# Linear attention with a mixture of experts: the attention's weights split by columns instead of by rows, k and q projected ahead of v

## The chip, the cores and the metric

The kernel runs on one core of a Trainium2 chip. The metric is the device time of one execution in microseconds (us). Three runs of the kernel before gave 1036.61, 1034.99 and 1036.34 us, median 1036.34.

## The reference

The input is x with 16 batches of 512 tokens and 256 features. For each batch the kernel computes:

```python
h = layernorm(x)
q, k, v = elu(h @ Wq.T) + 1, elu(h @ Wk.T) + 1, h @ Wv.T      # 16 heads of 16
num_i = q_i @ sum_{j<=i} k_j v_j^T ;  den_i = q_i . sum_{j<=i} k_j
x = x + (num / (den + 1e-8)) @ Wo.T
h = layernorm(x)
# router over 8 experts in 4 groups (best 2 groups, best 4 experts), weights cw
x = x + sum_e cw_e * (silu(h @ Wg_e) * (h @ Wu_e)) @ Wd_e + shared expert
```

## The kernel before, in words

Each batch is one tile: 512 tokens in four groups of 128. Every product of the projections and of the experts is computed with each float32 operand split into a high part and a remainder, three matmuls for one (`product`, line 989: high by high, high by low, low by high). ScalarE (ACT) makes the high part by a copy into a type of fewer bits, and VectorE (DVE) or GpSimd (POOL) the low part, the whole less the high part.

The order of the work on each engine is written out by hand in the tables `FIRST`, `STEP` and `LAST`: a word such as `k.0.0` is the step k, part 0, batch 0. Each engine goes through its own list strictly in order, and a step begins with the waits that its operands need. `FIRST` holds the start of the program and batches 0, 1 and part of 2; `STEP` is the pattern that repeats for batches 3 to 15; `LAST` is the end. The change touches `FIRST` alone.

The weights come as ten "pieces". SyncE's queue (SP) loads each into a staging buffer, ACT writes its high part (line 566), and POOL its low part (line 694), except piece 0, whose low part is DVE's (line 773). Pieces 0 and 1 are the attention's matrix `w_qkvo`, 256 rows in two blocks of 128 by 1024 columns (q, k, v and o, 256 columns each): before, piece n is row block n with all 1024 columns, in `cw_all`. Every projection sums over both row blocks, so each waits for both pieces. Pieces 2 to 6 are the experts' gate and up matrices, 7 to 9 the down matrices. The staging buffers of pieces 2 to 5 are those of `scores`, so no mask step of batch 0 may run before piece 5 has been split.

Steps of batch 0 that the prediction speaks of:

- `ln1_stats` (DVE, lines 749 to 757 and 783): means and variances, here that of batch 1 (`ln1_stats.0.1`), which stands in DVE's list directly ahead of `k.0.0`. After four `bn_stats` come small instructions on 128x4 elements. Three (752, 753, 754) are issued together and end in a wait for the third; then 755 and 756 together and a wait; then 757 and a wait; then 783 and a wait.
- `turn` (PE, line 1042): the normalized x transposed by TensorE; then ACT takes the high part (593) and DVE the low part (797).
- `warm.n` (PE, line 1034): n transposes that nobody reads; `WARM` is the number of such transposes ahead of the list (line 1003).
- `k`, `q` (PE, two row blocks by three matmuls of 512 columns; ACT relu at 624 and exp at 627; DVE at 816 writes `kf` or `qf`) and `v` (PE, twelve matmuls of 256 columns; ACT at 616). k has one scratch half of `expo` for both parts, so ACT's `k.1.0` waits until DVE has finished `k.0.0`; `q.1.0` on PE uses the bank of `q.0.0` and waits for DVE's `q.0.0`.
- `q_split` (ACT, 636), `scores` (PE, 1098), `mask` (DVE 860, or ACT 650 with POOL 720), `cum` (DVE scan, 853), `rstd1` (POOL, 699), which waits for `ln1_stats`.

Of the kernel before, what the change touches and what calls it, by code (L numbers as in the profile page):

```python
# [6 lines left out]
B, S, D = 16, 512, 256  # L7
# [9 lines left out]
KC = D // P  # L17
# [6 lines left out]

ET, HR, CW, SM, XB = 3, 3, 4, 8, 2
BANKS = 6
WARM = 16

# [33 lines left out]
}  # L64
FIRST = {
    "PE": """
        turn.0.0 turn.1.0 warm.17.0 v.1.0 k.0.0 q.0.0 v.0.0 k.1.0 q.1.0 scores.0.0 k_turn.0.0 scores.1.0
        warm.8.0 turn.0.1 turn.1.1 k_turn.1.0 state.0.0 values.0.0 scores.2.0 inter.0.0 values.1.0 scores.3.0
        k.0.1 q.0.1 inter.1.0 state.1.0 values.2.0 values.3.0 q.1.1 inter.2.0 scores.0.1 inter.3.0 warm.10.0
        k.1.1 wo.0.0 wo.1.0 scores.1.1 k_turn.1.1 v.1.1 v.0.1 k_turn.0.1 values.0.1 state.0.1 scores.2.1  # L70
# [3 lines left out]
        k_turn.1.2  # L74
        """,
    "ACT": """
        piece.0.0 piece.1.0 turn.1.0 turn.0.0 piece.2.0 v.1.0 piece.3.0 k.0.0 piece.4.0 piece.5.0 q.0.0 k.1.0
        q_split.0.0 q.1.0 mask.1.0 v.0.0 mask.3.0 k_turn.0.0 ln1_apply.0.1 mask.7.0 piece.6.0 turn.0.1
        turn.1.1 mask.5.0 q_split.1.0 k_turn.1.0 wide.0.0 mask.9.0 mask.11.0 mask.13.0 piece.7.0 mask.15.0
        k.0.1 q.0.1 wide.1.0 at.0.0 q_split.0.1 q.1.1 mask.1.1 mask.3.1 at.1.0 k.1.1 mask.5.1 mask.7.1  # L80
# [160 lines left out]
def linear_attention_moe(nc, x, w_qkvo, w_gate_up, w_down, w_router, bias, consts, out):  # L241
    f32, f32r = mybir.dt.float32, mybir.dt.float32r
    ALU, ACT, AX = mybir.AluOpType, mybir.ActivationFunctionType, mybir.AxisListType

    ctx = ExitStack()
    with ctx:
# [6 lines left out]
        def sem(name):  # L253
            return ctx.enter_context(nc.semaphore(name))


        wa_hi, wa_lo = (sb(f"wa_{n}", [P, KC, 4 * D], f32r) for n in ("hi", "lo"))
# [32 lines left out]
        scores = sb("scores", [P, SM, 4, P])  # L290
# [23 lines left out]
        warm = sb("warm", [P, SUBS])  # L314
# [21 lines left out]
        split_hi = sem("split_hi")  # L336
# [126 lines left out]
        def slot(b, e, n):  # L463
# [5 lines left out]
        staging = ([cw_all[:, 2 * j:2 * j + 2, :].rearrange("p a n -> p (a n)") for j in range(2)]  # L469
                   + [scores[:, 2 * j:2 * j + 2, :, :].rearrange("p a h n -> p (a h n)") for j in range(4)]  # L470
                   + [x_mid[1 - j][:, :, :].rearrange("p s d -> p (s d)") for j in range(2)])
        PIECES = [(w_qkvo[:, kc], 4 * D, wa_hi[:, kc], wa_lo[:, kc]) for kc in range(KC)]
        for s in range(0, SLOTS, 2):
            n = min(2, SLOTS - s)
            PIECES.append((w_gate_up[:, s * GU:(s + n) * GU], n * GU,
# [2 lines left out]
        for s in range(0, SLOTS, 4):  # L478
            n = min(4, SLOTS - s)
            PIECES.append((w_down[:, s * D:(s + n) * D], n * D,  # L480
                           wd_hi[:, s:s + n].rearrange("p s n -> p (s n)"),
                           wd_lo[:, s:s + n].rearrange("p s n -> p (s n)")))
        NP, NS = len(PIECES), len(staging)
        staged = [sem(f"staged{n}") for n in range(NP)]
        GATE_PIECE = [KC + i // 2 for i in range(SLOTS)]
        DOWN_PIECE = [KC + (SLOTS + 1) // 2 + i // 4 for i in range(SLOTS)]

        def wait_split(eng, n):

            if ("piece", n, 0) in SPLIT_DVE:  # L490
                wait_for(eng, attn_split, SPLIT_DVE["piece", n, 0])
            else:
                wait_for(eng, split_lo, SPLIT_POOL["piece", n, 0])
# [3 lines left out]
        @block.sync  # L497
        def _(sp):
            def load_x(b):

                wait_drained(sp, "wo", 0, b - XB)
                wait_drained(sp, "wo", 1, b - XB)
                if b == 0:
                    sp.dma_start(x_in[0][:, 0:HALF, :], x_v[0][:, 0:HALF, :]).then_inc(x_half, 16)
                    sp.dma_start(x_in[0][:, HALF:SUBS, :], x_v[0][:, HALF:SUBS, :]).then_inc(x_loaded[0], 16)
                else:
                    sp.dma_start(x_in[b % XB][:, :, :], x_v[b]).then_inc(x_loaded[b % XB], 16)

            for name, i, b in program("SP"):
                if name == "load_x":  # L510
                    load_x(b)
                elif name == "consts":
                    sp.dma_start(cst[:, :], consts).then_inc(small_in, 16)
                    sp.dma_start(bias_sb[:, :], bias.partition_broadcast(P)).then_inc(small_in, 16)
                    sp.dma_start(wr[:, :, :], w_router).then_inc(small_in, 16)
                elif name == "piece":
                    if i >= NS:
                        wait_split(sp, i - NS)
                    src, cols, _, _ = PIECES[i]
                    sp.dma_start(staging[i % NS][:, 0:cols], src).then_inc(staged[i], 16)  # L520
                elif name == "cw_store":
                    sp.wait_ge(cw_turned, b + 1)
                    for g in range(SUBS):
                        sp.dma_start(cw_dram[b % 2][:, g * P:(g + 1) * P], cw_t[RG * g:RG * g + E, :])\
                            .then_inc(cw_stored, 16)
                elif name == "cw_load":
                    sp.wait_ge(cw_stored, 64 * b + 64)
                    if b == 0:
                        wait_split(sp, NP - 1)
                    e = E * b + i - CW  # L530
                    if e >= 0:
                        wait_weighed(sp, e % E + int(e // E < B - 1), e // E)
                    sp.dma_start(cw_all[:, i % CW, :], cw_dram[b % 2, i].partition_broadcast(P))\
                        .then_inc(cw_loaded[i % CW], 16)
                elif name == "put":
                    sp.wait_ge(blocked, BLOCKED["blocks", i, b])
                    n = 2 * KC * (SUBS - 1) * P // 64 if i == 2 else SUBS * D // 32
                    for g in range(4):
                        rows, cs = slice(32 * g, 32 * g + 32), slice(32 * g, 32 * g + 32)
                        dst = (k_dram if i == 2 else x_dram[i])[b % 2].rearrange("(j t) d -> t j d", t=32)  # L540
                        sp.dma_start(dst[:, :, cs], blocks[rows, 0:32 * n].rearrange("t (j d) -> t j d", d=32))\
                            .then_inc(put_done, 16)
                elif name == "get":
                    sp.wait_ge(put_done, PUT["put", i, b])
                    if i == 2:
                        wait_filled(sp, "state", 0, b - 1)
                        wait_filled(sp, "state", 1, b - 1)
                        sp.dma_start(k_tok[:, :, :, :].rearrange("p m c d -> p (m c) d"),
                                     k_dram[b % 2].rearrange("(n p) d -> p n d", p=P)).then_inc(got[2], 16)
                    else:  # L550
                        sp.dma_start(landed[i].rearrange("p s k n -> p (s k) n"),
                                     x_dram[i][b % 2].rearrange("(n p) d -> p n d", p=P)).then_inc(got[i], 16)
                elif name == "store":
                    for j in range(2):
                        half = slice(j * HALF, (j + 1) * HALF)
                        sp.wait_ge(y_drained, Y_DRAINED["result", 0, b] - 1 + j)
                        sp.dma_start(out_v[b][:, half, :], x_mid[b % 2][:, half, :]).then_inc(out_sent[b % 2], 16)
            sp.wait_ge(out_sent[0], 32 * (B // 2))
            sp.wait_ge(out_sent[1], 32 * (B // 2))

        @block.scalar
        def _(act):
            def weights_high(n):
                _, cols, hi, _ = PIECES[n]
                act.wait_ge(staged[n], 16)
                nc.scalar.activation(hi, staging[n % NS][:, 0:cols], ACT.Copy).then_inc(split_hi, 1)


            act.wait_ge(zeros_set, 1)
# [115 lines left out]
        def _(pool):  # L685
# [4 lines left out]
            for name, i, b in program("POOL"):  # L690
                if name == "piece":
                    pool.wait_ge(split_hi, i + 1)
                    _, cols, hi, lo = PIECES[i]
                    nc.gpsimd.tensor_tensor(lo, staging[i % NS][:, 0:cols], hi.bitcast(f32), ALU.subtract)\
                        .then_inc(split_lo, 1)
                elif name == "rstd1":
                    pool.wait_ge(var1_ready, VAR1["ln1_stats", 0, b])
# [5 lines left out]
                elif name == "take":  # L703
                    pool.wait_ge(taken_hi, TAKEN_HI["take", i, b])
                    dst, hi = (xa_lo, xa_hi) if i < 2 else (xt_lo[b % 2], xt_hi[b % 2])
# [30 lines left out]
        def _(dve):  # L736
# [31 lines left out]

            for name, i, b in program("DVE"):
                if name == "piece":  # L770
                    _, cols, hi, lo = PIECES[i]
                    dve.wait_ge(split_hi, i + 1)
                    nc.vector.tensor_tensor(lo, staging[i][:, 0:cols], hi.bitcast(f32), ALU.subtract)\
                        .then_inc(attn_split, 1)
                elif name == "ln1_stats":
                    if b == 0:
# [17 lines left out]
                elif name == "turn":  # L794
                    dve.wait_ge(turn_hi, TURN_HI["turn", i, b])
                    dst, hi = (xa_lo, xa_hi) if i < 2 else (xt_lo[b % 2], xt_hi[b % 2])
# [22 lines left out]
                elif name == "blocks":  # L819
                    wait_blocks(dve, i, b)  # L820
                    if i == 0:
                        dve.wait_ge(norm1_ready, NORM1["ln1_apply", 0, b])
                        src = expo
                    elif i == 1:
                        dve.wait_ge(norm2_ready, NORM2["ln2_apply", 0, b])
                        src = num_t
                    else:
                        dve.wait_ge(drained[BANK["k", 0]], USES["k", 0, b])
                        dve.wait_ge(drained[BANK["k", 1]], USES["k", 1, b])
                        src = kf  # L830
                    n = (SUBS - 1) * P if i == 2 else S
# [153 lines left out]
        def _(pe):  # L985
# [18 lines left out]
            for name, i, b in program("PE"):  # L1004
# [40 lines left out]
                elif name in ("v", "wo"):  # L1045
# [3 lines left out]
                        wait_at(pe, 0, b)  # L1049
                        wait_at(pe, 1, b)  # L1050
                    if b == 0:
                        for n in range(KC):
                            wait_split(pe, n)
                    src = XA if name == "v" else AT
                    w0 = 2 * D if name == "v" else 3 * D
                    for j in range(2):
# [5 lines left out]
                elif name in ("k", "q"):  # L1062
                    w0 = (D if name == "k" else 0) + i * P
                    wait_normal(pe, 0, b)
                    if b == 0:
                        for n in range(KC):
                            wait_split(pe, n)
                    for kc in range(KC):
                        last = product(bk[:, :], cols(WA, ALL, kc, slice(w0, w0 + P)),
                                       cols(XA, ALL, kc, ALL), kc == 0, kc == KC - 1)  # L1070
# [130 lines left out]
```

## Time and profile before

| | |
|---|---|
| runs | 1034.99, 1036.34, 1036.61 us |
| profiled execution | 1035.56 us, span 1033.8 us |
| busy: PE, DVE, POOL, ACT | 1007.7, 873.0, 537.8, 422.6 us |
| chain that ended last | PE 87%, DVE 6%, DMA 2%, ACT 1%, POOL 1% |

The span runs from the first to the last instruction; 1.76 us of the execution lie around it. Busy time is the time in which the engine had an instruction in work. The chain that ended last is followed back from the last instruction to what released each step.

### The profile page before, as it was taken

To read this page: it belongs to the slowest core of one execution; us is meant where nothing else is said; L and a number is where in the kernel's file an instruction comes from. 1 tells how busy PE (TensorE), PEld (TensorE's weight loads), DVE (VectorE), ACT (ScalarE), POOL (GpSimd) and SP (SyncE) were. 2 spreads that over 40 slices of the span, in tenths; PEclk is the share of its full clock that TensorE was granted. 3 is DMA by queue.
4 is the path that set the end of the run, shared out by engine and by line. 5 is a ranking of instruction groups with operands and counts; after the bars stand their busy time and mean duration, and the time that the engine had idled before them with its cause. 6 is when DMAs were issued, how large, how long until landed. Compare 5 with 4: busy or idle time off the path is not lost.

```text
span 1033.8 us, 22214 instructions
## 1 busy us (share of the span) xinstructions
PE 1007.7 (97%) x8437; PEld 858.1 (83%) x8437; DVE 873.0 (84%) x1855; ACT 422.6 (41%) x750; POOL 537.8 (52%) x440
## 2 busy tenths in 40 slices
PE   6889999999999999999999999999999999999997
PEld 5667878888888888888888888888888888888886
DVE  5988998898888889989898988889889898887564
ACT  5755343443434344343444434244343434422222
POOL 5763545636455564445646454564445546443653
PEclk9999999999999999999999999999999999999999
DMA  5011424444242443324435252443424345241511
GB/s 204 2 47 43 106 60 133 83 103 111 60 138 63 132 105 96 100 63 134 83 103 113 58 138 63 142 94 99 100 64 136 76 103 113 58 118 36 130 60 64
DMA packets 235161, 96.49 MB, mean 93 GB/s; under 512 B 161712, under 2 KB 217520, under 8 KB 235056
## 3 DMA queue, kind: packets, MB, share of 16 engines
q1 hardware_dynamic: 235056, 95.07, 36.0%
q8 instruction: 68, 1.11, 0.5%
q14 instruction: 37, 0.30, 0.1%
HBM read 66.60 MB, written 28.44 MB: 92 GB/s over the span
## 4 chain that ended last, share of the span: by engine, by line
PE 87%; DVE 6%; DMA 2%; ACT 1%; issue 1%; POOL 1%; SPq 1%; DVEq 0%; ACTq 0%
PE bank L989 53%; PE y_bank L989 19%; PE bank L1098 6%; PE bank L1114 5%; PE bank L1085 2%; PE bank L1128 2%; PE bank L1140 1%; DMA cw_all<-cw_dram 1%; DMA cw_all<-in_w_qkvo 1%; DVE scores L860 1%; DMA x_dram<-blocks 0%; DMA expo<-x_dram 0%; DVE den L869 0%; POOL et L729 0%; DVE et L957 0%
## 5 line engine op out<-in xcount | busy, mean ns | idle before, releaser
L989 PE MATMUL bank<-xt_hi,wg_hi 128*128 128x512 f32 x576 | 237.1, 412 | 3.0 <-DVE et L957 2.3
L989 PE MATMUL bank<-xt_hi,wg_lo 128*128 128x512 f32 x576 | 228.1, 396 | 0.0
L989 PE MATMUL bank<-xt_lo,wg_hi 128*128 128x512 f32 x576 | 227.8, 396 | 0.0
L732 POOL TENSOR_TENSOR h_lo<-et,h_hi 128x512 fp32r<-128x512 f32 x142 | 181.1, 1293 | 89.6 <-ACT h_hi L682 89.4
L729 POOL TENSOR_TENSOR et<-et,cw_all 128x512 f32<-128x512 f32 x126 | 166.2, 1338 | 112.6 <-DVE et L963 94.4
L860 DVE TENSOR_TENSOR scores<-bank,cst 128x512 f32<-128x512 f32 x240 | 152.6, 681 | 35.6 <-PE bank L1098 29.4
L989 PE MATMUL y_bank<-wd_hi,h_hi 128*128 128x256 f32 x576 | 164.9, 286 | 0.0
L989 PE MATMUL y_bank<-wd_lo,h_hi 128*128 128x256 f32 x576 | 162.1, 281 | 0.0
L989 PE MATMUL y_bank<-wd_hi,h_lo 128*128 128x256 f32 x576 | 161.3, 280 | 0.0
L989 PEld LDWEIGHTS bank<-xt_hi,wg_hi 128*128 128x128 f32 x576 | 108.3, 188 | 41.3 <-issue 16.6
L682 ACT ACTIVATE h_hi<-et 128x512 fp32r<-128x512 f32 x144 | 86.1, 624 | 116.7 <-POOL et L729 55.9
L957 DVE SCALAR_TENSOR_TENSOR et<-et,bank 128x512 f32<-128x512 f32 x144 | 95.9, 677 | 40.8 <-ACT et L673 40.7
L989 PEld LDWEIGHTS bank<-xt_hi,wg_lo 128*128 128x128 f32 x576 | 108.4, 188 | 26.0
L717 POOL TENSOR_TENSOR cum<-cum,qf 128x512 f32<-128x512 f32 x32 | 41.2, 1286 | 161.7 <-DVE qf L816 157.2
L989 PEld LDWEIGHTS bank<-xt_lo,wg_hi 128*128 128x128 f32 x576 | 108.8, 189 | 19.7
L673 ACT ACTIVATE et<-bank 128x512 f32<-128x512 f32 x144 | 82.1, 592 | 91.2 <-PE bank L989 58.4
L989 PEld LDWEIGHTS y_bank<-wd_hi,h_hi 128*128 128x128 f32 x576 | 108.5, 188 | 7.5 <-issue 4.0
L989 PEld LDWEIGHTS y_bank<-wd_lo,h_hi 128*128 128x128 f32 x576 | 108.4, 188 | 2.8
L989 PEld LDWEIGHTS y_bank<-wd_hi,h_lo 128*128 128x128 f32 x576 | 108.6, 189 | 0.0
L963 DVE SCALAR_TENSOR_TENSOR et<-et,bank 128x512 f32<-128x512 f32 x144 | 95.0, 678 | 13.5 <-PE bank L989 9.7
L636 ACT ACTIVATE q_half<-qf,cst 128x512 f32<-128x512 f32 x64 | 42.6, 714 | 118.3 <-PE bank L1098 117.6
L1098 PE MATMUL bank<-q_half,kf 32*128 32x256 f32 x1024 | 73.3, 400 | 2.8 <-DVE st L839 1.1
(135 smaller groups left out, 1870.5 us busy)
## 6 DMA issues: line engine op xcount, KB each, us to landing
cw_all<-cw_dram SPq DMA_DIRECT2D x128, 256.0 KB, 3.9
x_dram<-blocks SPq DMA_DIRECT2D x112, 128.0 KB, 3.3
out_y<-x_mid SPq DMA_DIRECT2D x32, 256.0 KB, 4.8
x_in<-in_x SPq DMA_DIRECT2D x15, 512.0 KB, 5.3
num_t<-x_dram SPq DMA_DIRECT2D x15, 512.0 KB, 4.0
expo<-x_dram SPq DMA_DIRECT2D x13, 512.0 KB, 4.0
k_dram<-blocks SPq DMA_DIRECT2D x52, 96.0 KB, 2.6
k_tok<-k_dram SPq DMA_DIRECT2D x13, 384.0 KB, 3.4
```

Of the source, the lines that this page charges most:

```text
L636: nc.scalar.activation(q_half[:, j, :], qf[:, i, :], ACT.Copy, scale=cst[:, C_EO + j:C_EO + j + 1]).then_inc(q_half_done, 1)
L673: nc.scalar.activation(et[:, i % ET, :], bank[BANK["gate", i]][:, :], ACT.Tanh, scale=0.5)\
L682: nc.scalar.activation(h_hi[:, i % HR, :], et[:, i % ET, :], ACT.Copy).then_inc(h_hi_done, 1)
L717: nc.gpsimd.tensor_tensor(cum[:, i, :], cum[:, i, :], qf[:, i, :], ALU.mult).then_inc(qk_done, 1)
L729: nc.gpsimd.tensor_tensor(et[:, i % ET, :], et[:, i % ET, :], weights, ALU.mult).then_inc(weighed, 1)
L732: nc.gpsimd.tensor_tensor(h_lo[:, i % HR, :], et[:, i % ET, :], h_hi[:, i % HR, :].bitcast(f32), ALU.subtract).then_inc(h_lo_done, 1)
L860: nc.vector.tensor_tensor(scores[:, i % SM, :, :], bank[BANK["scores", i]][:, :].rearrange("p (h q) -> p h q", h=4), causal.unsqueeze(1).b ...
L957: nc.vector.scalar_tensor_tensor(et[:, i % ET, :], et[:, i % ET, :], 1.0, bank[BANK["gate", i]][:, :], ALU.add, ALU.mult)\
L963: nc.vector.scalar_tensor_tensor(et[:, i % ET, :], et[:, i % ET, :], 0.5, bank[BANK["up", i]][:, :], ALU.mult, ALU.mult)\
L989: ins = nc.tensor.matmul(dst, l, r, start=first and n == 0, stop=last and n == 2, skip_group_check=shared)
L1098: last = nc.tensor.matmul(bank[BANK["scores", 4 * i + g]][:, j * 2 * P:(j + 1) * 2 * P] .rearrange("p (h q) -> p h q", h=2), kf[rows, m, c ...
L1114: last = nc.tensor.matmul(bank[BANK["o", m]][32 * g:32 * g + 32, c * P:(c + 1) * P], v_win[:, c, 4 * m + g, h:h + 2, :].rearrange("p t d - ...
```

## The change

The weights' pieces 0 and 1 become column blocks: piece 0 holds the columns of q and k of both row blocks, piece 1 those of v and o. Both have as many bytes as before. k and q wait for piece 0 alone, v and o for piece 1 alone. PE projects k and q ahead of v, ACT takes the turns ahead of piece 1 and v after q, and 9 + 10 unread transposes take the place of 16 + 17.

```diff
-WARM = 16
+WARM = 9
 FIRST["PE"]:
-        turn.0.0 turn.1.0 warm.17.0 v.1.0 k.0.0 q.0.0 v.0.0 k.1.0 q.1.0 scores.0.0 k_turn.0.0 scores.1.0
+        turn.0.0 turn.1.0 warm.10.0 k.0.0 q.0.0 v.1.0 v.0.0 k.1.0 q.1.0 scores.0.0 k_turn.0.0 scores.1.0
 FIRST["ACT"]:
-        piece.0.0 piece.1.0 turn.1.0 turn.0.0 piece.2.0 v.1.0 piece.3.0 k.0.0 piece.4.0 piece.5.0 q.0.0 k.1.0
+        piece.0.0 turn.1.0 turn.0.0 piece.1.0 piece.2.0 piece.3.0 k.0.0 piece.4.0 piece.5.0 q.0.0 v.1.0 k.1.0
-        PIECES = [(w_qkvo[:, kc], 4 * D, wa_hi[:, kc], wa_lo[:, kc]) for kc in range(KC)]
+        PIECES = [(w_qkvo[:, :, n * 2 * D:(n + 1) * 2 * D], KC * 2 * D, wa_hi[:, :, n * 2 * D:(n + 1) * 2 * D],
+                   wa_lo[:, :, n * 2 * D:(n + 1) * 2 * D]) for n in range(2)]
+        def stage(n):
+            flat = staging[n % NS][:, 0:PIECES[n][1]]
+            return flat.rearrange("p (k n) -> p k n", k=KC) if n < KC else flat
 v, wo (PE):
                     if b == 0:
-                        for n in range(KC):
-                            wait_split(pe, n)
+                        wait_split(pe, 1)
 k, q (PE):
                     if b == 0:
-                        for n in range(KC):
-                            wait_split(pe, n)
+                        wait_split(pe, 0)
```

The lists of DVE, POOL and SP stay as they were. In the loads and splits `stage(n)` takes the place of the flat staging buffer.

## Rows read from the trace of the kernel before

**Rows 1.** Busy time by stretch of the span: us, engines, clock, DMA.

```profile
14.60:90.00 75.40, 65.48 (x692) 52.51 (x693) 65.80 (x134) 48.62 (x87) 49.37 (x35) 1.00 0.10 36
150.00:950.00 800.00, 798.00 (x6744) 681.60 (x6743) 699.65 (x1498) 321.03 (x573) 409.05 (x334) 1.00 0.39 98
```

**Rows 2.** Timeline of PE at the start: start, duration, instructions.

```profile
6.95 3.67 PE L1003 MATMUL bank<-cst 128*128 128x128 f32 x16 [6.95 <-DMA wr<-in_w_router]
...
10.42 1.44 PE L1042 MATMUL bank<-cst,expo 128*128 128x128 f32 x8
...
11.70 2.02 PE L1034 MATMUL y_bank<-cst 128*128 128x128 f32 x17
...
14.62 0.36 PE L989 MATMUL bank<-wa_hi,xa_hi 128*128 128x256 f32 x1 [0.90 <-POOL wa_lo L694]
```

**Rows 3.** The chain that ended last, in order of time: start, duration, step.

```profile
12.11 2.38 POOL wa_lo L694
...
22.91 1.67 PE bank L989 x6
...
24.65 1.24 PE bank L1098 x16
```

**Rows 4.** Timeline of ACT at the start.

```profile
11.94 1.06 ACT L593 ACTIVATE xa_hi<-bank 128x512 fp32r<-128x512 f32 x2
...
16.39 0.60 ACT L616 ACTIVATE v_win<-bank 128x512 f32<-128x512 f32 x1 [2.44 <-PE bank L989]
16.89 1.05 ACT L566 ACTIVATE wg_hi<-scores 128x1024 fp32r<-128x1024 f32 x1
17.84 0.59 ACT L624 ACTIVATE expo<-bank 128x512 f32<-128x512 f32 x1
...
19.00 1.99 ACT L566 ACTIVATE wg_hi<-scores 128x1024 fp32r<-128x1024 f32 x2
...
22.04 0.58 ACT L624 ACTIVATE expo<-bank 128x512 f32<-128x512 f32 x1
...
23.18 1.32 ACT L636 ACTIVATE q_half<-qf,cst 128x512 f32<-128x512 f32 x2
```

**Rows 5.** Timeline of DVE at the start.

```profile
7.61 1.38 DVE L790 TENSOR_SCALAR expo<-x_in,rstd,shift 128x256 f32<-128x256 f32 x4 [1.56 <-POOL shift L701]
10.85 1.23 DVE L773 TENSOR_TENSOR wa_lo<-cw_all,wa_hi 128x1024 fp32r<-128x1024 f32 x1 [1.86 <-ACT wa_hi L566]
12.55 1.29 DVE L797 TENSOR_TENSOR xa_lo<-bank,xa_hi 128x512 fp32r<-128x512 f32 x2 [0.47 <-ACT xa_hi L593]
...
15.23 1.62 DVE L752 TENSOR_TENSOR m_sum<-stats 128x4 f32<-128x4 f32 x1
...
19.19 0.69 DVE L816 SCALAR_TENSOR_TENSOR kf<-bank,expo 128x512 f32<-128x512 f32 x1 [1.52 <-ACT expo L627]
...
23.92 2.26 DVE L853 TENSOR_TENSOR_SCAN cum<-cst,kf 128x512 f32<-128x512 f32 x1
```

**Rows 6.** Timeline of POOL at the start: the pieces' low parts.

```profile
14.44 2.39 POOL L694 TENSOR_TENSOR wg_lo<-scores,wg_hi 128x1024 fp32r<-128x1024 f32 x1
18.02 7.09 POOL L694 TENSOR_TENSOR wg_lo<-scores,wg_hi 128x1024 fp32r<-128x1024 f32 x3 [1.18 <-ACT wg_hi L566]
```

**Rows 7.** Timeline of DVE at 137 us: the router's small instructions.

```profile
137.40 0.84 DVE L930 TENSOR_TENSOR sig_c<-sig,bias_sb 128x32 f32<-128x32 f32 x1
138.27 1.28 DVE L932 TENSOR_TENSOR g_sum<-sig_c 128x16 f32<-128x16 f32 x1
139.58 1.25 DVE L762 TENSOR_TENSOR compare<-g_sum 128x64 f32<-128x64 f32 x1
```

**Rows 8.** Timeline of POOL at 137 us.

```profile
138.22 2.52 POOL L706 TENSOR_TENSOR xa_lo<-expo,xa_hi 128x512 fp32r<-128x512 f32 x2
```

**Rows 9.** DMAs issued at 4.6 and 5.3 us: KB each, us from issue to landing.

```profile
x_in<-in_x SPq DMA_DIRECT2D x1, 512.0 KB, 9.2
...
scores<-in_w_gate_up SPq DMA_DIRECT2D x1, 512.0 KB, 9.7
```

More of the change, by code:

```diff
@@ L518, in _ @@
                         wait_split(sp, i - NS)
-                    src, cols, _, _ = PIECES[i]
-                    sp.dma_start(staging[i % NS][:, 0:cols], src).then_inc(staged[i], 16)
+                    sp.dma_start(stage(i), PIECES[i][0]).then_inc(staged[i], 16)
                 elif name == "cw_store":
@@ L563, in weights_high @@
             def weights_high(n):
-                _, cols, hi, _ = PIECES[n]
                 act.wait_ge(staged[n], 16)
-                nc.scalar.activation(hi, staging[n % NS][:, 0:cols], ACT.Copy).then_inc(split_hi, 1)
+                nc.scalar.activation(PIECES[n][2], stage(n), ACT.Copy).then_inc(split_hi, 1)
             act.wait_ge(zeros_set, 1)
@@ L692, in _ @@
                     pool.wait_ge(split_hi, i + 1)
-                    _, cols, hi, lo = PIECES[i]
-                    nc.gpsimd.tensor_tensor(lo, staging[i % NS][:, 0:cols], hi.bitcast(f32), ALU.subtract)\
+                    _, _, hi, lo = PIECES[i]
+                    nc.gpsimd.tensor_tensor(lo, stage(i), hi.bitcast(f32), ALU.subtract)\
                         .then_inc(split_lo, 1)
@@ L770, in _ @@
                 if name == "piece":
-                    _, cols, hi, lo = PIECES[i]
+                    _, _, hi, lo = PIECES[i]
                     dve.wait_ge(split_hi, i + 1)
-                    nc.vector.tensor_tensor(lo, staging[i][:, 0:cols], hi.bitcast(f32), ALU.subtract)\
+                    nc.vector.tensor_tensor(lo, stage(i), hi.bitcast(f32), ALU.subtract)\
                         .then_inc(attn_split, 1)
```

## The prediction

> **What bounds the kernel now.** I read the busy time by stretch first. From 150 to 950 us PE is busy for 798.0 of 800 us: the reader should see there that the steady state is PE's and that the change, which touches only the start, adds or removes nothing in it. From 14.6 to 90 us PE is busy for 65.48 of 75.4 us, so some 10 us of waits lie there [rows 1]. Whatever comes earlier or later at the start therefore reaches the end one for one, unless one of these waits takes it up.
>
> Next I read the front on PE. Sixteen unread transposes begin at 6.95, when the constants have landed; the turns follow at 10.42, seventeen more transposes at 11.70, and the first projection begins at 14.62, released by POOL's low part of piece 1 [rows 2]. The chain confirms it: POOL at 12.11 for 2.38 us; and it shows the next marks, the projection q.1 at 22.91 (six matmuls, 1.67 us) and the first scores at 24.65 [rows 3]. I take that start of the scores, 24.65, as the measure of the front.
>
> Between 14.62 and 24.65 the engine without a gap is ACT: v.1 at 16.39 after 2.44 us idle for PE, then piece 3 (1.05), k.0 (17.84 to 19.00, so 1.2 for a relu with its exp), pieces 4 and 5 (1.99), q.0, k.1 at 22.04, and q_split at 23.18 for 1.32, which releases the scores at 24.5 [rows 4]. DVE waits for ACT in that stretch (kf at 19.19, 1.52 idle) [rows 5].
>
> The row that matters most is a small one: at 15.23 DVE's m_sum, 4 elements a partition, takes 1.62 us [rows 5]. It ends at 16.85, as POOL's subtraction for piece 2 does (14.44 + 2.39 = 16.83); then POOL is idle until 18.02, for want of piece 3's high part [rows 6], and the other small instructions of these statistics pass.
>
> **The change part by part.**
>
> *Fewer unread transposes ahead.* Sixteen take 3.67 us, nine some 2.0: they end near 8.9. The normalized x is ready at 7.61 + 1.38 = 8.99 [rows 5], so the turns come from 10.42 to about 9.05. Sixteen transposes in 3.67 us against seventeen in 2.02 [rows 2] is the difference between TensorE's lower and its higher clock; the early ones run at the lower. So the turns will take 8 x 0.21 = 1.7 us and not 1.44, and end near 11.0 where they ended at 11.86: 0.9 us won. The ten transposes behind them end near 12.2 and wait for nobody.
>
> *Columns instead of rows; turns ahead of piece 1.* Piece 0's low part starts on DVE at 10.85 for 1.23, as before; DVE's two turns follow at once (12.0 to 13.3, by their 1.29 us [rows 5]), since ACT's turns run at about 11.05 instead of 11.94 [rows 4]. k.0 waits for these alone and starts at 13.35 instead of 14.62 for the first projection: 1.25 us won. Splitting the load in runs of half the length moves the same bytes. I put it at 0; no row shows the same load in both forms, and the bounds are a gain of 0.1 and a loss of 0.3 us.
>
> *ACT without its wait for v.* Piece 1 follows the turns (12.0 to 13.1), piece 2 to 14.1. Piece 3 was issued at 5.3 and landed 9.7 later, at 15.0 [rows 9], so it runs 15.05 to 16.1. Then k.0 to 17.3, pieces 4 and 5 to 19.2, q.0 to 20.4, v.1 to 20.9. By ACT alone k.1 would start at 20.9 and not 22.04, and the scores would come 1.2 us sooner.
>
> *What this does to POOL and DVE.* POOL's piece 1 starts at 13.1 instead of 12.11. Its later pieces have their high parts long before POOL is free (14.1, 16.1, 18.3, 19.2 against 15.5, 17.9, 20.2, 22.6), so POOL runs five subtractions with no gap, 7.09 / 3 = 2.36 us each [rows 6]: ends at 15.5, 17.85, 20.2, 22.6 and 24.95. The gap from 16.83 to 18.02, through which DVE's statistics passed, is gone. Batch 1's x landed at 4.6 + 9.2 = 13.8 [rows 9], so m_sum comes again at 15.2, while piece 1 is being subtracted, and waits until 15.5.
>
> What happens to the rest is shown by the router at 137 us: of a chain of small dependent instructions with two inputs in SBUF, each waits for one POOL instruction to end, passes, and the next, issued some 0.03 us later, meets the following one: 0.84, 1.28 and 1.25 us, while POOL runs back to back [rows 7, 8]. The statistics are four such stages (three instructions, two, one, one). With one stage at each of POOL's ends they finish at 15.5, 17.9, 20.2 and 22.6, not at 17.7. Behind them in DVE's list stands k.0, which was at 19.19: now it starts at 22.65 and ends at 23.35. For q.0 DVE was late anyway (its exp is ready at 20.4); it ends at 24.0.
>
> The Trainium skill, SBUF — State Buffer, section Who interferes with whom, says a DVE instruction with two SBUF inputs, or in a two-port mode, and a GpSimd instruction that reads SBUF exclude each other for a whole instruction. The trace agrees at 15.23 and 137 us. Without the rule, by instruction counts only, the sum would be the gain of 1.2 us above.
>
> *The sum.* ACT's k.1 needs DVE's k.0 out of `expo`: it starts at 23.35 instead of 22.04 and ends 24.55; q_split takes 1.32, to 25.9. PE's q.1 needs q.0's bank: 24.05 + 1.67 = 25.75, inside that. Scores at 26.0 against 24.65: **+1.35 us**. DVE's scan, which stood behind piece 5 (23.92, 2.26 us [rows 5]), now stands behind POOL's rstd and comes about 1.1 later. For the waits between 26 and 90 us I take no change; bounds: a gain of 0.7 (POOL is then early relative to DVE, so less of the den steps' waiting) and a loss of 0.5. The profiled execution took 1035.56, so 1036.9 for its like; the median of the runs is 0.78 above it: **1037.7 us**.
>
> **The rivals.**
>
> *A. One of the small instructions issued together needs an end of its own.* At an end of POOL only the waiting instruction may get through, not the two behind it. For that: POOL's next one takes the turn at once in [rows 7, 8]. Against: those were 0.03 us late, whereas 753 follows 752 before its end. One more stage brings the statistics to 24.95, where POOL runs out of pieces and its rstd waits for DVE itself, so that is also the limit. kf then ends at 25.7, k.1 at 26.9, q_split at 28.2: +3.7 us. PE, having ended k.1 near 20.6, stands idle 5.8 us until q.1 (forecast: 3.4). The trace shows PE at its lower clock after its idle start; if it falls back there, q.1 and the scores (1.67 + 1.24 us) take up to twice as long. Between +3.7 and +6: I take +4.7, 1041.0 us. It decides from the point where 754 misses the end at 15.5.
>
> The Trainium skill, TensorE: Matmul & The Clock Gate, Part 1, says a TensorE that has idled falls to 1.2 GHz and regains 2.4 GHz only after sustained work. No idle stretch inside this span is as long as rival A's, so the trace cannot show whether it would.
>
> *B. The statistics get through and the front's gain stays.* If DVE keeps its turn over a chain of small instructions, ACT decides: 1.2 us won, 1035.1 us. For it: k.0 and q.0 are done 2 to 3 us earlier on PE. Against it: rows 7. A more lucky meeting of DVE and POOL behind the front could add 1 us.
>
> *C. The later waits take up the loss, or the gain.* With 10 us of waits of PE up to 90 us this is possible; 1036.3 us. Against: in that stretch the chain goes on through DVE, whose work all hangs on the scores.
>
> **How the numbers follow.** Forecast 42%, A 28%, B 17%, C 13%. A measurement tells about 0.2% (2.1 us) from no change. The forecast lies inside that, but for a quarter of it or so (the clock, 1 us or more on top); A outside; B inside but for its lucky part; C inside. That gives slower 0.37, same 0.54, faster 0.09. The range for 8 in 10: below to B's 1035.1 less the 0.3 of spread, 1034.8; above over A's own value, to 1041.6.
>
> **What would show it.** In the trace after: the first projection near 13.35 (else the front's sum is wrong); POOL's five subtractions end to end from 13.1 to 25.0; DVE's lines 752, 755 or 756, 757 and 783 of batch 1 with durations over 1 us, each ending where one of POOL's ends; kf near 22.65 and ACT's second relu of k at 23.35; the scores near 26.0. kf before 20.5 would mean B; kf near 25 would mean A, and transposes or matmuls at double spacing behind it the lower clock. If the scores come at 26.0 but the time is 1036 or less, C is right. The forecast is wrong as a whole if POOL has a gap among its pieces, as then the statistics pass early.

## The result and the profile after

Seven runs of the changed kernel took 1038.64 to 1042.18 us, median 1040.26, against 1036.34 before; the ratio is 1.0039 (95% interval 1.0026 to 1.0053). The profiled execution took 1038.81 us, its span 1037.0. The time lies inside the range of the prediction, but above the 1037.7 us that it gave: what happened is rival A (chance 28%), whose 1041.0 it nearly is. Two slow runs stand in none of the ratios: 3445.65 us, of the kernel before, and 1096.53 us, of the kernel with fifteen more unread transposes.

Busy time by stretch of the changed kernel (us, then PE, PEld, DVE, ACT, POOL, granted clock, DMA share, GB/s), to be held against [rows 1]:

```profile
14.60:90.00 75.40, 61.88 (x637) 48.99 (x636) 66.96 (x119) 46.06 (x82) 48.59 (x35) 0.95 0.09 34
150.00:950.00 800.00, 798.51 (x6704) 681.97 (x6706) 703.44 (x1498) 321.95 (x575) 408.91 (x334) 1.00 0.40 98
15.00:20.00 5.00, 5.00 (x35) 4.59 (x34) 4.97 (x4) 4.62 (x8) 5.00 (x3) 1.00 0.60 233
20.00:25.00 5.00, 1.29 (x6) 0.71 (x4) 4.93 (x4) 0.42 (x1) 5.00 (x3) 1.00 0.00 0
25.00:30.00 5.00, 3.45 (x11) 2.35 (x15) 3.28 (x5) 2.94 (x5) 2.17 (x4) 0.50 0.00 0
```

The steady state is PE's as before. From 20 to 25 us PE and ACT stand nearly still, while DVE seems busy for 4.93 us with four instructions. Those are the small ones of the statistics. DVE's timeline of the changed kernel (start, duration), which answers to [rows 5]; lines 758 to 763 and 789 are 752 to 757 and 783 of before:

```profile
11.90 1.29 DVE L803 TENSOR_TENSOR xa_lo<-bank,xa_hi 128x512 fp32r<-128x512 f32 x2 [0.69 <-ACT xa_hi L599]
13.11 1.39 DVE L755 BATCH_NORM_STATS2 stats<-x_in 128x6 f32<-128x256 f32 x4
14.53 1.26 DVE L758 TENSOR_TENSOR m_sum<-stats 128x4 f32<-128x4 f32 x1
15.72 0.15 DVE L759 TENSOR_TENSOR m_dif<-stats 128x4 f32<-128x4 f32 x1
15.80 2.37 DVE L760 TENSOR_TENSOR v_sum<-stats 128x4 f32<-128x4 f32 x1
18.20 2.34 DVE L761 SCALAR_TENSOR_TENSOR m_dif<-m_dif 128x4 f32<-128x4 f32 x1
20.47 0.16 DVE L762 TENSOR_SCALAR v_sum<-v_sum 128x4 f32<-128x4 f32 x1
20.66 2.21 DVE L763 TENSOR_TENSOR veps<-m_dif,v_sum 128x4 f32<-128x4 f32 x1
22.90 2.27 DVE L789 TENSOR_SCALAR minus_mean<-m_sum 128x4 f32<-128x4 f32 x1
25.20 0.69 DVE L822 SCALAR_TENSOR_TENSOR kf<-bank,expo 128x512 f32<-128x512 f32 x1
25.81 0.68 DVE L822 SCALAR_TENSOR_TENSOR qf<-bank,expo 128x512 f32<-128x512 f32 x1
```

And POOL's, which answers to [rows 6]:

```profile
13.38 2.40 POOL L700 TENSOR_TENSOR wa_lo<-cw_all,wa_hi 128x1024 fp32r<-128x1024 f32 x1 [5.66 <-ACT wa_hi L572]
15.72 9.42 POOL L700 TENSOR_TENSOR wg_lo<-scores,wg_hi 128x1024 fp32r<-128x1024 f32 x4
25.25 1.01 POOL L705 TENSOR_TENSOR rstd<-veps,power 128x4 f32<-128x4 f32 x1
```

The reader is to see the same moments in both: POOL's first subtraction ends at 15.78 and the four behind it follow without a gap, one every 2.36 us or so. Five of DVE's instructions on four elements a partition last until one of these ends: 15.79, 18.17, 20.54, 22.87 and 25.17. m_dif passed with m_sum at the first end; v_sum, which started 0.08 us later, did not, and took the second. Only then could the chain 761, 763, 789 go on. kf starts at 25.20, not at 19.19 [rows 5]. Not all of those that waited have two inputs in SBUF: 789 reads `m_sum` alone and took 2.27 us. kf, one of whose two inputs is a PSUM bank, took 0.69 us at 19.19 in the kernel before, in the midst of POOL's row.

ACT's and PE's timelines show who waits for it; to be held against [rows 4] and [rows 2, 3]:

```profile
11.27 1.08 ACT L599 ACTIVATE xa_hi<-bank 128x512 fp32r<-128x512 f32 x2 [1.39 <-PE bank L1048]
...
25.99 0.60 ACT L630 ACTIVATE expo<-bank 128x512 f32<-128x512 f32 x1 [5.57 <-DVE kf L822]
...
27.16 1.32 ACT L642 ACTIVATE q_half<-qf,cst 128x512 f32<-128x512 f32 x2
```

```profile
6.48 2.18 PE L1009 MATMUL bank<-cst 128*128 128x128 f32 x9 [6.48 <-DMA wr<-in_w_router]
9.26 1.97 PE L1048 MATMUL bank<-cst,expo 128*128 128x128 f32 x8 [0.60 <-DVE expo L796]
11.02 2.34 PE L1040 MATMUL y_bank<-cst 128*128 128x128 f32 x10
13.24 0.80 PE L995 MATMUL bank<-xa_hi,wa_hi 128*128 128x512 f32 x1
...
26.55 0.80 PE L995 MATMUL bank<-xa_hi,wa_hi 128*128 128x512 f32 x1 [5.26 <-DVE qf L822]
27.14 0.63 PE L995 MATMUL bank<-xa_lo,wa_hi 128*128 128x512 f32 x1
...
29.41 2.09 PE L1102 MATMUL bank<-q_half,kf 32*128 32x256 f32 x16
```

ACT was free at 20.4 and took up k.1 at 25.99. PE ended its projections at 21.3, stood idle for 5.26 us, and came back at half its clock: the granted clock of 25 to 30 us is 0.50, 1.2 instead of 2.4 GHz, q.1 takes 2.86 us (26.55 to 29.41) where it took 1.74 (22.91 to 24.65), and the scores 2.09 where the same view of the kernel before has 1.15 (the 1.24 of [rows 3] is the chain's, up to the next step). The first scores start at 29.41, not at 24.65. The next mark, the scores of the second half of the heads, stood at 34.52 before and stands at 39.67, 5.15 us late. PE's timeline, before and then after:

```profile
34.52 1.15 PE L1098 MATMUL bank<-q_half,kf 32*128 32x256 f32 x16 [1.13 <-DVE st L839]
```

```profile
39.67 1.15 PE L1102 MATMUL bank<-q_half,kf 32*128 32x256 f32 x16 [0.55 <-ACT k_tok L647]
```

The difference of the profiled spans is 3.2. It was still 5.3 us at 132 us, and 1.6 us of it went between 132 and 152 us (5.28 at 132, 3.66 at 152): from 142 to 153 us the kernel before had 1.6 us of waits of PE for DVE, and this one had none. PE's waits of the kernel before in that stretch (total, times, longest):

```profile
PE bank L989 <- DVE qf L816: 1.0, 1, 1.0
PE bank L989 <- DVE et L957: 0.6, 1, 0.6
```

Of the traces of the ten other kernels below, all but one (the gap taken away in the kernel before) also gain 1.4 to 2.3 us on the kernel before in that stretch, whatever their front. So this part does not hang on what the change does to the front.

### The profile page after: what moved, and what is told of

The parts are those of the page before. It is cut to its first block, busy times and chain, and to the rows that moved or that the text cites. A ratio compares the mean times of both kernels' runs of the same rounds, so it can differ in the third digit from the quotient of the medians.

```text
span 1037.0 us, 22185 instructions
## 1 busy us (share of the span) xinstructions
PE 1009.2 (97%) x8423; PEld 858.8 (83%) x8423; DVE 882.0 (85%) x1855; ACT 423.0 (41%) x750; POOL 537.1 (52%) x440
## 4 chain that ended last, share of the span: by engine, by line
PE 90%; DVE 6%; DMA 1%; issue 1%; ACT 1%; POOL 1%; SPq 0%; DVEq 0%; ACTq 0%; POOLq 0%
PE bank L995 54%; PE y_bank L995 19%; PE bank L1102 6%; PE bank L1118 5%; PE bank L1089 2%; PE bank L1132 2%; PE bank L1144 1%; DMA cw_all<-cw_dram 1%; POOL et L735 0%; DVE scores L866 0%; DVE den L875 0%; DVE xa_lo L803 0%; DMA x_in<-in_x 0%; DVE stats L755 0%; DVE den L874 0%
```

## The experiments

Two theories stand against each other. Theory 1: POOL's subtractions without a gap hold back DVE's statistics, and with them k, ACT and PE; TensorE's clock adds to it. Theory 2: the fewer unread transposes, the new order of the projections or the new form of the loads cost the time, and the statistics are beside it. In the lists, `...` stands for words left out. Each ratio is to the kernel before, run on the same chip. "First scores" and "second half" are the two marks, 24.65 and 34.52 in the kernel before, 29.41 and 39.67 in the changed one.

### The statistics moved behind k.1

```diff
 FIRST["DVE"] of the changed kernel:
-... turn.1.0 turn.0.0 ln1_stats.0.1 k.0.0 q.0.0 k.1.0 cum.0.0 q.1.0 ...
+... turn.1.0 turn.0.0 k.0.0 q.0.0 k.1.0 ln1_stats.0.1 cum.0.0 q.1.0 ...
```

> The changed kernel with one word moved: DVE's ln1_stats.0.1 behind k.1.0 instead of ahead of k.0.0. Theory 1 (POOL's five subtractions without a gap hold back the small instructions of the statistics, and k.0 behind them): kf starts near 17.5 instead of 25.2, the first scores near 23.4 instead of 29.4, PE's idle stretch ahead of q.1 shrinks from 5.3 us to under 1.5 and the granted clock stays 1.00 from 20 to 30 us; the time is 4 to 6 us under the changed kernel's, at 1034.5 to 1036. Theory 2 (fewer unread transposes and the new order of the projections cost the time through TensorE's clock, the statistics are beside it): the time stays within 1 us of 1040.

Measured: median 1035.54 us, ratio 1.0009 (0.9995 to 1.0023). DVE's timeline of this kernel:

```profile
17.00 0.69 DVE L822 SCALAR_TENSOR_TENSOR kf<-bank,expo 128x512 f32<-128x512 f32 x1 [3.96 <-ACT expo L633]
...
24.68 0.34 DVE L758 TENSOR_TENSOR m_sum<-stats 128x4 f32<-128x4 f32 x1
24.95 0.15 DVE L759 TENSOR_TENSOR m_dif<-stats 128x4 f32<-128x4 f32 x1
25.02 0.15 DVE L760 TENSOR_TENSOR v_sum<-stats 128x4 f32<-128x4 f32 x1
```

POOL's row of subtractions is as gapless as in the changed kernel (13.22 to 25.00), yet kf starts at 17.00; the statistics, arriving at the row's end, pass within 1.2 us. One word in DVE's list takes the loss from 0.39% down to 0.09%, which is not clear of nothing. The first scores came at 23.98, the second half at 35.89, 1.4 us later than in the kernel before: the front's gain was lost again because the statistics now stand ahead of scan and masks. PE waited 2.0 us for the masks,

```profile
28.40 1.86 PE L1102 MATMUL bank<-q_half,kf 32*128 32x256 f32 x16 [1.98 <-DVE scores L866]
```

and came back at the lower clock for a time (granted clock 0.79 from 30 to 35 us; these scores took 1.86 us, not 1.15). This rules theory 2 out for all but small parts: all that it names is still in this kernel, and the interval ends at 0.23%.

### The transposes of before in the changed kernel

```diff
-WARM = 9
+WARM = 16
-turn.0.0 turn.1.0 warm.10.0 k.0.0 ...
+turn.0.0 turn.1.0 warm.17.0 k.0.0 ...
```

> The changed kernel with the unread transposes of before (16 and 17). Theory 1: k.0 may start a little later, up to 14.6, and at the higher clock, but kf still starts near 25.2, the idle stretch and the lower clock behind it stay, and the time stays at 1039 to 1042. Theory 2: the time falls to 1036 to 1037.5.

Measured: median 1041.28 us, ratio 1.0055 (1.0037 to 1.0073). PE's first projection came at 13.37 (13.24 in the changed kernel), the idle stretch was 6.1 us, the granted clock 0.50 again, the second half at 39.98. The transposes are not where the time went.

### The gap taken away in the kernel before

```diff
 FIRST["ACT"] of the kernel before:
-... turn.0.0 piece.2.0 v.1.0 piece.3.0 k.0.0 ...
+... turn.0.0 piece.2.0 piece.3.0 v.1.0 k.0.0 ...
```

> The kernel before with one word moved: ACT takes piece.3.0 ahead of v.1.0, so that POOL has no gap between pieces 2 and 3; rows, transposes and the order on PE as before. Theory 1: the five POOL subtractions run from 12.1 to 24 without a gap, m_sum passes at 16.8, the later stages at 19.2, 21.5 and 23.9, kf starts near 24 instead of 19.2, the scores near 28, and the time is 3 to 5.5 us over before, 1039.5 to 1042. Theory 2: no change, 1036 to 1037.

Measured: median 1035.10 us, ratio 0.9998 (0.9985 to 1.0010). Theory 1's numbers were wrong here and theory 2's right. DVE's and POOL's timelines say why:

```profile
15.37 1.67 DVE L752 TENSOR_TENSOR m_sum<-stats 128x4 f32<-128x4 f32 x1
16.96 2.42 DVE L753 TENSOR_TENSOR m_dif<-stats 128x4 f32<-128x4 f32 x1
19.31 0.15 DVE L754 TENSOR_TENSOR v_sum<-stats 128x4 f32<-128x4 f32 x1
...
19.97 0.17 DVE L783 TENSOR_SCALAR minus_mean<-m_sum 128x4 f32<-128x4 f32 x1
20.17 0.69 DVE L816 SCALAR_TENSOR_TENSOR kf<-bank,expo 128x512 f32<-128x512 f32 x1
```

```profile
14.61 4.75 POOL L694 TENSOR_TENSOR wg_lo<-scores,wg_hi 128x1024 fp32r<-128x1024 f32 x2
20.19 4.75 POOL L694 TENSOR_TENSOR wg_lo<-scores,wg_hi 128x1024 fp32r<-128x1024 f32 x2 [0.82 <-ACT wg_hi L566]
```

With the gap between pieces 2 and 3 closed, m_dif missed the first end and waited 2.4 us, as the lock-out has it. But a gap of 0.82 us opened one piece later, since ACT still had v.1 and k.0 ahead of piece 4; all the rest passed through it. kf came 1.0 us late, and ACT, which set the pace there, did not need it sooner (first scores at 24.75, second half at 34.34). I had taken the row of POOL to be gapless without working out when piece 4's high part would be ready. So the loss needs a row with no gap at all until the end, which the changed kernel makes by taking v off ACT's way.

### The idle stretch filled

```diff
 FIRST["PE"] of the changed kernel:
-... v.0.0 k.1.0 q.1.0 scores.0.0 ...
+... v.0.0 k.1.0 warm.46.0 q.1.0 scores.0.0 ...
```

> The changed kernel with 46 unread transposes put between k.1.0 and q.1.0 on PE, which fill the idle stretch from 21.3 to 26.5 us. Theory 1 with a surcharge by the clock: kf still starts near 25.2, the granted clock stays at 1.00 from 25 to 30 us in place of 0.50, q.1 (six matmuls) takes 1.7 us instead of 2.9 and the scores 1.2 instead of 2.1; the time falls by 1.5 to 2.5 us, to 1038 to 1039, not to before's. If the clock has no part in it: no change. If it is all of it: 1036.

Measured: median 1038.83 us, ratio 1.0038 (1.0022 to 1.0055). kf stayed at 25.01. The clock's part in the front is shown: the granted clock of 25 to 30 us is 1.00 instead of 0.50, the first scores take 1.15 us,

```profile
28.42 1.15 PE L1102 MATMUL bank<-q_half,kf 32*128 32x256 f32 x16 [0.41 <-ACT q_half L642]
```

and the second half starts at 37.72, 1.95 us sooner than in the changed kernel. The time does not show it: the median fits the expectation, the ratio is that of the changed kernel. The profiled execution can't say why: it is the slowest of the ten, 1044.56 us, and no other went over 1041.01. In it a load of x issued at 59.19 took 5.5 us to land where it took 3.8 in the changed kernel. DVE waited 2.23 us for it, PE then stood idle for 2.29 us from 65.58, and after that the granted clock fell (0.66 from 67.5 to 70 us); the difference to the kernel before grew there from 3.2 to 7.1 us. What the other nine executions do in that place is not known, so the 2 us are shown for the front and not for the whole.

### A gap for the statistics on POOL

```diff
 FIRST["POOL"] of the changed kernel:
-rstd1.0.0 piece.1.0 piece.2.0 piece.3.0 piece.4.0 piece.5.0 rstd1.0.1 qk.0.0 ...
+rstd1.0.0 piece.1.0 rstd1.0.1 piece.2.0 piece.3.0 piece.4.0 piece.5.0 qk.0.0 ...
```

> The changed kernel with one word moved on POOL: rstd1.0.1 behind piece.1.0 instead of behind piece.5.0. POOL then waits for the statistics after its first subtraction, which opens a gap. Theory 1 (lock-out by back-to-back subtractions): m_sum passes near 15.5, all the others within 0.6 us behind it, kf starts near 17.0 and the first scores near 24, as when the statistics stand behind k.1; but pieces 2 to 5 end near 26.3 instead of 25.1 and the masks with them, so the time is 1035.5 to 1037.5, 3 to 4 us under the changed kernel's. Theory 2 (clock and order of the projections): 1039 to 1041.

Measured: median 1037.35 us, ratio 1.0017 (1.0006 to 1.0028). DVE's list is that of the changed kernel; its timeline:

```profile
14.81 0.58 DVE L758 TENSOR_TENSOR m_sum<-stats 128x4 f32<-128x4 f32 x1
15.31 0.15 DVE L759 TENSOR_TENSOR m_dif<-stats 128x4 f32<-128x4 f32 x1
15.39 0.15 DVE L760 TENSOR_TENSOR v_sum<-stats 128x4 f32<-128x4 f32 x1
...
16.05 0.17 DVE L789 TENSOR_SCALAR minus_mean<-m_sum 128x4 f32<-128x4 f32 x1
16.96 0.69 DVE L822 SCALAR_TENSOR_TENSOR kf<-bank,expo 128x512 f32<-128x512 f32 x1 [0.74 <-ACT expo L633]
...
27.86 1.29 DVE L866 TENSOR_TENSOR scores<-bank,cst 128x512 f32<-128x512 f32 x2 [3.23 <-POOL wg_lo L700]
```

The instructions, their place in DVE's list and the five subtractions are the same; only POOL's pause, and its rstd within it, is new, and the small ones pass in 1.4 us (14.81 to 16.22) where they took 10.6 (14.53 to 25.17). That is the lock-out shown from POOL's side. The price came where it was expected, and larger: the pieces ended at 27.8, not near 26.3. POOL's pause lasted from 15.37 to 17.54, and the lock-out works the other way too: DVE's scan began at 22.18, and the subtraction that POOL began at 22.25 took 3.28 us instead of 2.4. So the masks waited 3.23 us, PE stood idle for 4.46 us and came back at the lower clock (0.56 from 30 to 35 us). The first scores came at 22.91, but the second half at 37.74, 1.9 us sooner than in the changed kernel and 3.2 later than before.

### Two pieces given to DVE

Against the kernel with the gap on POOL:

```diff
 FIRST["POOL"]:
-... piece.1.0 rstd1.0.1 piece.2.0 piece.3.0 piece.4.0 piece.5.0 qk.0.0 ...
+... piece.1.0 rstd1.0.1 piece.2.0 piece.4.0 qk.0.0 ...
 FIRST["DVE"]:
-... ln1_stats.0.1 k.0.0 q.0.0 k.1.0 cum.0.0 ...
+... ln1_stats.0.1 k.0.0 piece.3.0 q.0.0 k.1.0 piece.5.0 cum.0.0 ...
 mask of batch 0 (ACT, DVE): waits for piece 4 as well as piece 5
```

> As the kernel with the gap on POOL, and pieces 3 and 5 subtracted by DVE (behind k.0 and behind k.1) instead of POOL. Theory 1: statistics at 15.5 to 16.1, kf near 17, the last piece subtracted near 24.5 instead of 26.3, scores and masks 1 us earlier than before's: 1033.5 to 1035.5, the fastest so far. If DVE's two subtractions are themselves held up by POOL's (two SBUF inputs each): piece 5 at 25.5 to 27 and 1035.5 to 1037.

Measured: median 1033.77 us, ratio 0.9987 (0.9977 to 0.9997). kf at 16.67, piece 5 subtracted by

```profile
22.14 2.18 DVE L780 TENSOR_TENSOR wg_lo<-scores,wg_hi 128x1024 fp32r<-128x1024 f32 x1
```

which waited 1 us for POOL's piece 4 and ended at 24.3; first scores at 22.86, second half at 34.16.

### The same with fifteen more unread transposes

```diff
-... k.1.0 q.1.0 scores.0.0 k_turn.0.0 ...
+... k.1.0 q.1.0 warm.7.0 scores.0.0 warm.8.0 k_turn.0.0 ...
```

> The kernel with the gap on POOL and pieces 3 and 5 on DVE, with 7 unread transposes ahead of scores.0.0 and 8 behind it. In the run without them PE was idle 0.8 and 1.0 us there and the granted clock fell to 0.75 over 25 to 30 us. If the clock costs something there: granted clock 1.00 from 25 to 35 us, the marks at 34 us some 0.5 to 1 us earlier and the time 0.5 to 1 us less, 1033. If not: no change, or up to 0.5 us more, as the transposes end late.

Measured: median 1034.90 us, ratio 0.9988 (0.9976 to 1.0000). Busy time from 25 to 30 us, without them and then with them:

```profile
25.00:30.00 5.00, 3.82 (x28) 3.04 (x29) 4.13 (x7) 4.33 (x9) 4.47 (x4) 0.75 0.01 3
```

```profile
25.00:30.00 5.00, 3.95 (x43) 3.41 (x42) 4.33 (x8) 4.97 (x11) 4.57 (x4) 1.00 0.00 0
```

The granted clock stays up and the second half starts at 32.88 instead of 34.16. In the time of all runs (median 1034.90 us) the 1.3 us don't show.

### The parts of the change that stay

Columns alone (the pieces, each projection's own wait; all lists and the transposes as before):

> The weights by columns alone: pieces 0 and 1 are column blocks, each projection waits for its own, all lists and the 16 and 17 unread transposes are those of before. The loads have runs of half the length. Theory 1: v.1 still starts when POOL's piece 1 is done, POOL keeps its gap before piece 3, kf near 19.2, and the time is before's, 1035 to 1036.5. If the shorter runs cost transfer time: pieces 0 and 1 land later by up to 0.3 us each and all of the front with them, 1036.5 at most. Theory 2 (the loads are a large part of the loss): 1038 or more.

Measured: median 1034.46 us, ratio 0.9987 (0.9977 to 0.9997); marks at 24.67 and 34.56, as before. DVE's first split starts at 10.84 (before 10.85 [rows 5]). So the loads by columns cost the front nothing here, as the forecast had it; SyncE took longer to issue them (1.30 us for the two instead of 0.91), which held nothing up in the first 35 us. Its first 35 us are those of before, yet its ratio is the same 0.9987 as that of the kernel with two pieces on DVE.

Fewer transposes alone, in the kernel before:

> The kernel before with 9 and 10 unread transposes in place of 16 and 17, nothing else. The first projection still waits for POOL's piece 1 at 14.6, but PE has done less ahead of it. Theory 1 with the clock as a small part: the twelve matmuls of v.1 run at double spacing for part of their 1.6 us, v.1's eviction and all of ACT behind it come 0.5 to 1 us later, the time is 1036.3 to 1037. Theory 2: 1039 to 1040.

Measured: median 1034.71 us, ratio 0.9992 (0.9983 to 1.0002). Here PE was idle 1.8 us ahead of v.1, and its clock fell while v.1 ran (granted clock 0.66 from 15 to 20 us). The marks are 1.7 and 1.3 us late (26.30, 35.81). The expected loss in time (1036.3 to 1037) did not come, though the front is late.

More transposes with the statistics behind k.1:

> The kernel with the statistics behind k.1, and 16 and 17 unread transposes. There ACT waited 0.9 us for k.1 of PE, whose first four matmuls had run at double spacing. With more transposes: PE's first projection at 14.3 at the higher clock, or at 13.3 if the transposes are done by then; the granted clock unchanged. Either gain or loss under 0.7 us against the same kernel with 9 and 10: 1035 to 1036.5.

Measured: median 1036.45 us, ratio 1.0002 (0.9990 to 1.0013); second half at 35.87 where it was 35.89. The first scores came 1.5 us sooner (22.50 instead of 23.98), but the masks still waited for POOL's row, which ended at 24.37, and for the statistics, so nothing of it is left at the second mark.

## Why the prediction was right and where it was wrong

*The start on PE and ACT*: right. The first projection came at 13.24 (13.35 forecast), ACT's turns at 11.27 (11.05). Two parts were missed, and both hid under the longer wait. PE's clock rose only at about 14.8, after its first three matmuls (in the trace before it had risen by 11.7 [rows 2]); so the turns took 1.97 us and not 1.7, and the ten transposes ended at 13.36 and not near 12.2, just as the turns' low part was ready (11.90 + 1.29). That is not fixed by their number: in the kernel with the gap on POOL the same ten took 1.25 us instead of 2.34. And piece 0 came sooner than assumed: DVE's split began at 9.98, not at 10.85. It began at 9.4 to 10.5 in all kernels with the changed kernel's list on ACT and at 10.8 to 11.1 in the others; why is open.

*POOL without a gap, and DVE's statistics behind it*: right in mechanism. The five subtractions ran from 13.38 to 25.14 (13.1 to 24.95 forecast).

*"With one stage at each of POOL's ends they finish at 15.5, 17.9, 20.2 and 22.6"*: this is the step that failed, and the term of the sum mis-sized by it is the start of k.0 on DVE, 22.65 in the forecast and 25.20 in the trace. It took the three instructions issued together to pass at one end. m_dif did, v_sum did not; so five ends were needed, and the statistics finished at 25.17. Elsewhere it fell out otherwise: with the gap closed in the kernel before, m_dif already missed. In the changed kernel 762 passed with 761; in the one with 16 and 17 transposes it did not:

```profile
20.61 2.38 DVE L762 TENSOR_SCALAR v_sum<-v_sum 128x4 f32<-128x4 f32 x1
```

What passes lies within 0.1 us of an end, and I cannot say from these runs what decides it. The forecast should have put the likelier value on more ends.

*The sum*: q_split ended at 28.5, the first scores came at 29.41. Of those 4.76 us, 3.7 had been worked out for rival A without the clock (28.35); the rest is the clock of q.1 (28.42 with the idle stretch filled). The scores at the lower clock made it 5.73 at the next scores (33.40 for 27.67), of which 0.58 were regained by the second mark at 39.67.

*The clock*: named as a surcharge of rival A alone, "between +3.7 and +6", and that is what the front shows, +5.15. After 5.26 us idle PE was at 1.2 GHz; with the stretch filled it was not, and 1.95 us came back at the second mark. The Trainium skill, TensorE: Matmul & The Clock Gate, Part 1, says that TensorE falls to 1.2 GHz once it has been idle, and here the runs agree. The forecast itself had 3.4 us of idle PE and took nothing for it, without a reason: in the kernel with the statistics behind k.1 and more transposes, idle stretches of 1.4 and 2.2 us were followed by a granted clock of 0.58 from 25 to 30 us.

*From the front to the end, one for one*: only roughly. +5.15 us at 40 us became +3.2 in the profiled spans and 0.39% (4.0 us) over all runs. Part is the 1.6 us that PE waited between 142 and 153 us in the profiled execution of before. The kernel with columns alone has the same marks to 0.05 us and gained 1.9 us on it there, so those waits are not given by the front. What decides them stays open. Held against columns alone, the changed kernel is slower by 1.0039 / 0.9987, 0.52% or 5.4 us (an estimate from two ratios, each good to about 0.1%), which is the front's 5.15 nearly one for one. That the time came out so close to rival A's 1041.0 is in part luck: the front cost 5.15 us where A took 4.7, and a stretch that A says nothing of gave 1.6 us back. Fewer transposes alone show how loose the tie is at 1 us: marks 1.3 us late, and no loss.

*Rival B*: the front's gain was really there for the taking (first scores at 22.86 with the statistics let through), but not in the changed kernel. *Rival C* took up a part, as above.

*The best version.* Against the changed kernel, two pieces on DVE with a pause on POOL save 0.5% (0.9987 / 1.0039), and so do columns alone. Against the kernel before, 0.9987 is clear of 1 by its interval, but columns alone reach it with an unchanged front. I therefore don't claim that its 0.13% come from the front.

## What to carry to other kernels

When an engine's wait is removed, look at who used the pause: here POOL's idle 1.2 us were the only time in which DVE's chain of small instructions on SBUF (most with two inputs, but 762 and 789 with one were held too) could run, and an earlier high part from ACT, whose list no longer had v in the way, closed it. Count such a chain in the other engine's whole instructions (here 2.36 us each, and five ends) and place it where that engine waits anyway, or make it wait. And when a start is rearranged for 1 us, look for the idle stretch it can open on TensorE, since the lower clock behind it is charged on top.

## What else the runs showed

The column of granted clock reads 1.00 before PE's first work and through 15 us, while 128x128 transposes and the first matmuls of 512 columns follow one another at twice the spacing they have later (0.43 against 0.23 us): at the start of a program the spacing tells the clock, not the column.

Idle stretches well under 5 us also came ahead of the lower clock: 1.8 us ahead of v.1 with few transposes in front of it (0.66 from 15 to 20 us), and, with two pieces on DVE, pauses of 0.8, 1.0 and 1.1 us with little work between them (0.75 from 25 to 30 us), where 15 unread transposes kept it at 1.00. The single runs of one kernel spread over 2 to 9 us, more than most of the differences under study.
